# Identity multiplies on TensorE ahead of 22 waits in the first two sequences and the last one of a transformer block

## The reference, cut to what matters

```
x = x + attention0(layernorm(x))        # 16 heads of 8, full softmax, no output projection
x = x + ffn0(layernorm(x))              # 128 -> 512 relu -> 128
x = x + attention1(layernorm(x))        # 16 heads of 8, rotary, causal, output projection
x = x + local(layernorm(x))             # two layers; each: shift half of the features by a token,
                                        #   8 heads of 64 in a window of 64, then a gated gelu FFN
```

## Time and profile before

| what | us |
|---|---|
| median of 3 runs | 3026.3 |
| the profiled execution's own time | 3027.28 |
| its span, first to last instruction | 3025.5 |
| PE busy (share of the span) | 2775.7 (92%) |
| DVE busy | 2343.5 (77%) |
| ACT busy | 2138.3 (71%) |
| POOL busy | 1608.1 (53%) |
| mean granted clock of PE | 0.965 |

### The profile page before, as it was taken

The page is one execution under the profiler, slowest core; times in us unless marked ns, Lnnn a source line. Parts: engine busy times, 40 slices in busy tenths (PEclk is TensorE's granted clock), DMA queues, the critical chain, the costliest instruction groups (busy, mean ns, idle before and its releaser), DMA issues.

```text
span 3025.5 us, 66249 instructions
## 1 busy us (share of the span) xinstructions
PE 2775.7 (92%) x22656; PEld 1931.4 (64%) x22656; DVE 2343.5 (77%) x6016; ACT 2138.3 (71%) x5956; POOL 1608.1 (53%) x1747
## 2 busy tenths in 40 slices
PE   4688999999999999999999999999999999998875
PEld 2455666666676666666666666666666666666653
DVE  3467878888888888888888888887888888877753
ACT  2356777777777877777787777777777777776653
POOL 1045555566555556655555665555566555546642
PEclk7689999999999999999999999999999999999997
DMA  2000000000000000000000000000000000000000
GB/s 70 3 3 4 7 5 7 4 7 6 7 7 5 7 4 7 6 6 7 7 5 4 7 6 6 7 6 5 4 7 7 6 7 7 5 4 5 5 5 5
DMA packets 41976, 21.79 MB, mean 7 GB/s; under 512 B 21130, under 2 KB 41012, under 8 KB 41652
## 3 DMA queue, kind: packets, MB, share of 16 engines
q1 hardware_dynamic: 41652, 17.55, 2.1%
HBM read 9.17 MB, written 4.19 MB: 4 GB/s over the span
## 4 chain that ended last, share of the span: by engine, by line
PE 44%; ACT 23%; DVE 15%; POOL 7%; issue 3%; DMA 0%; DVEq 0%; POOLq 0%; SPq 0%; ACTq 0%
DVE negmax L864 7%; ACT P L756 6%; ACT rawP L756 6%; PE bank L1176 6%; PE bank L1192 5%; PE bank L1083 4%; PE bank L1184 4%; PE bank L1129 3%; PE bank L1118 3%; POOL rn L654 3%; PE bank L1163 3%; PE bank L1151 2%; ACT P L739 2%; PE bank L1063 2%; PE bank L1164 2%
## 5 line engine op out<-in xcount | busy, mean ns | idle before, releaser
L864 DVE TENSOR_REDUCE negmax<-bank 128x2 f32<-128x512 f32 (+1 forms) x896 | 559.9, 684 | 26.6 <-PE bank L1044 25.0
L723 ACT ACTIVATE probs<-bank 128x384 f32<-128x384 f32 (+1 forms) x1024 | 481.2, 581 | 110.3 <-PE bank L1063 109.1
L599 POOL TENSOR_TENSOR veps<-moments,eps_tile 128x2 f32<-128x2 f32 x192 | 38.4, 200 | 768.7 <-DVE moments L816 768.7
L1118 PE MATMUL bank<-wqkv_sb,hS 128*128 128x512 f32 x768 | 397.2, 625 | 27.0 <-DVE rawP L914 8.6
L621 POOL TENSOR_SCALAR_AFFINE_SELECT probs<-probs 128x256 f32<-128x256 f32 x512 | 245.9, 508 | 300.3 <-ACT probs L723 300.1
L654 POOL TENSOR_TENSOR rn<-ss_kept,minus_half 128x16 f32<-128x16 f32 x128 | 372.6, 2911 | 13.4 <-DVE ss_kept L921 12.8
L942 DVE TENSOR_REDUCE negmax<-bank 128x2 f32<-128x384 f32 (+1 forms) x384 | 212.9, 596 | 133.1 <-PE bank L1151 125.5
L1083 PE MATMUL bank<-probs,V 128*16 128x256 f32 (+1 forms) x4096 | 255.5, 369 | 24.8 <-ACT probs L723 22.8
L642 POOL TENSOR_TENSOR rawA<-rawA,rope_sb 128x512 f32<-128x512 f32 x128 | 164.6, 1286 | 168.4 <-ACT rawA L742 167.4
L1044 PE MATMUL bank<-kT,qT 32*128 32x256 f32 (+1 forms) x2048 | 213.4, 325 | 22.8 <-DVE negmax L864 17.2
L756 ACT ACTIVATE rawP<-bank,negmax 128x128 f32<-128x128 f32 x512 | 180.2, 378 | 66.8 <-DVE negmax L942 66.7
(11 more groups left out here) (139 smaller groups left out, 7283.4 us busy)
## 6 DMA issues: line engine op xcount, KB each, us to landing
xin<-x SPq DMA_DIRECT2D x32, 128.0 KB, 5.0
out<-xout SPq DMA_DIRECT2D x32, 128.0 KB, 1.8
V<-YB SPq DMA_DIRECT2D x64, 63.5 KB
wqkv_sb<-wqkv SPq DMA_DIRECT2D x1, 1536.0 KB
V<-YB SPq DMA_DIRECT2D x64, 0.2 KB
w_sb<-w SPq DMA_DIRECT2D x1, 682.0 KB
w_sb<-w SPq DMA_DIRECT2D x2, 256.0 KB, 3.0
wo_sb<-wo SPq DMA_DIRECT2D x2, 256.0 KB
```

The costliest lines, as they stand in the source:

```text
L723: nc.scalar.activation(dst, src, ACT.Exp, scale=SCALE0 if k == ATTN0 else SCALE1)\
L864: nc.vector.reduce_max(negmax[:, k, t, head:head + 4 * many - 3:4], tile(u, e)[:, :].rearrange("p (h k) -> p h k", h=many), AX.X, negate=T ...
L1118: mm(tile(u)[:], hS[:, l, t * P:(t + 1) * P], wqkv2_sb[:, l, m * INNER:(m + 1) * INNER], start=True, stop=True).then_inc(has_filled(u), 1)
```

## The change

A table gives a number of filler matmuls for 21 entries (sequence, stream, unit kind, part). Two entries match two units each (`turn_q` part 0, plain and with the maxima; `turn` of sequence 1, for the attention and for the FFN) and the very first `turn` of sequence 0 is left out. Ahead of such a unit PE waits until that unit's own bank is free, then multiplies the identity by four copies of itself (128x128 by 128x512, fp32r) into that bank as often as the table says, raising no semaphore. After that the unit waits for its inputs as before and overwrites the bank. There are 46 fillers in sequence 0, 48 in sequence 1, 22 in LOCAL0 and 70 in LOCAL1 of sequence 31, 186 in all.

```diff
+FILLERS = {
+    (0, ATTN0): {("turn_q", 0): 5, ("mix", 0): 7, ("mix", 1): 7, ("mix", 2): 7, ("mix", 3): 7, ("turn", 0): 8},
+    (1, ATTN0): {("turn_q", 0): 5, ("mix", 0): 7, ("mix", 1): 7, ("mix", 2): 7, ("mix", 3): 7, ("turn", 0): 5},
+    (31, LOCAL0): {("qkv2", 4): 6, ("scores2", 2): 6, ("turn_p", 0): 10},
+    (31, LOCAL1): {("qkv2", 2): 24, ("turn_q2", 0): 9, ("turn_p", 0): 9, ("turn", 0): 28},
+}
 NBANKS = 8
...
+                fillers = FILLERS.get((u.sequence, k), {}).get((u.kind, u.part), 0)
+                if fillers and (u.number > 2 or u.sequence > 0):
+                    for sem, count in newest(free(u)):
+                        pe.wait_ge(sem, count)
+                    for _ in range(fillers):
+                        mm(tile(u)[:].rearrange("p (a k) -> p a k", a=4), ident_r[:],
+                           ident_r[:].unsqueeze(1).broadcast_to([P, 4, P]), start=True, stop=True, skip_group_check=True)
+
                 if u.kind in ("turn", "shift"):
```

## The result

| kernel | median us | lowest and highest | runs | ratio to before, 95% interval |
|---|---|---|---|---|
| before, in these measurements | 3026.86 | 3024.83 to 3030.24 | 8 | |
| with the change | 3036.23 | 3028.83 to 3038.14 | 8 | 1.0027 [1.0016, 1.0038] |

What follows compares the result with a forecast made beforehand. PE bounds the whole span (92% busy), but where fillers lie no engine is full and a chain between engines counts. Sequences 0 and 1 about +1, the end +3.6: 3026.3 + 4.6 = 3030.9 us, range 3024 to 3038.

Steps and rivals of the forecast that it cites:

- The mechanism: In about half the places the bank holds the fillers back to the pause's end, so the pause stays.
- The price of a filler: On PE, each uncovered filler costs 0.427 us at half clock and 0.236 at full clock.
- Rival 2: Every filler shows its weight load, 0.315 or 0.575 us each: about +12 more, 3042 us; chance 0.15.
- Sequence 0, +5: Fillers of sequence 0 at the start cost about 5 us, passed on whole to sequence 1.
- sequence 1, -4.2: Most banks are free early in sequence 1; fillers cost little and full clock gives more back: sum -4.2 us.
- LOCAL0, +1.1: Sequence 31, LOCAL0: fillers of `qkv2` 4 +1.3, `scores2` 2 +1.42, `turn_p` 0 +0.1, return -1.7; net +1.1 us.
- what follows runs at full clock: -1.7: In LOCAL0, work behind the fillers of `turn_p` 0 was to run at full clock, returning 1.7 us.
- LOCAL1, +2.5: Sequence 31, LOCAL1: +1.9 up to the scores, `turn_p` 0 +2.5 less 1.4, `turn` -0.5; net +2.5 us.
- Rival 1: The clock stays up once the first fillers have run, in all four stretches: 3018.6 us; chance 0.15.
- Rival 3: The clock does not rise by fillers: sequence 0 +14, sequence 1 +5, the end +17, 3062 us; chance 0.05.
- Rival 4: Nothing shows: fillers lie under other work and the clock is unchanged, 3026 us; chance 0.1.
- Three signs named ahead: Sequence 1 later; 8.4 us pause ahead of the `qkv2` 2 fillers, `turn_q2` some 5 later; spacing 0.43 or 0.22 to 0.24.

Runs made afterwards that it cites:

- start alone: Changed kernel with only the fillers of sequences 0 and 1 kept, in their own banks: 3028.48 us against 3026.76 before, ratio 1.0002 [0.9992, 1.0012].
- the 24 in a free bank: Only the 24 fillers ahead of `qkv2` 2 of LOCAL1 kept, in the bank used longest ago: 3025.40 us against 3026.25 before, ratio 0.9996.

## Why the prediction was right in sign and short in size

**The mechanism: right.** The step was that a filler's own bank is freed by the releaser of the pause in about half the places. The rows after show it at each place named (17.97, 39.76, 2968.59), and the run with free banks changes nothing but the bank, and with it this wait, and moves the time from +0.3% to -0.4%. In LOCAL0 free banks take back only the cost of the six fillers of `qkv2` 4 (+0.2 for +1.3).

**The price of a filler: right.** Inside a chain of fillers the starts lie 0.427 us apart at half clock and 0.224 to 0.24 at full clock, which are the values taken. Only the first distance of a chain is longer, as a rule some 0.59 and 0.335. From the first of the 24 to the `qkv2` behind them are 7.56 us, with the clock rising during the tenth, and 6.96 in two other profiles, where it rises during the seventh. 7.4 was forecast with nine; that number had no row behind it, and it came out near. Rival 2, a load shown by every filler (0.575 and 0.315), falls: only the first distance of a chain is as long as that. The Trainium skill's figure of 131 ns for each pair of a sustained stream (same page, section Back-to-back issue gap) doesn't hold for these in fp32r: 0.224 is the smallest distance here.

**Sequence 0, +5, and sequence 1, -4.2: right as far as can be told.** Sequence 0 alone is +4.8 by its ratio, with 3 us on either side, and +1.6 to +5.6 in four profiles, of which up to 1.5 is the spread at that mark. Sequence 1 is -3.0 to -5.3 in the profiles. Their sum was forecast at +1; start alone is +0.6 by its ratio, with an interval of 3 us on either side.

**LOCAL0, +1.1: wrong, the step that failed.** It measured +5.6. Its parts:

| part | forecast | measured (three profiles) |
|---|---|---|
| six fillers of `qkv2` 4 | +1.3 | +1.2 to +1.4 |
| `scores2` 2 and `turn_p` 0, with what follows at full clock | -0.2 | +1.1 to +1.3 |
| one or both `up2` at half clock | 0 | +2.8 to +3.1 |

The fillers' own cost was about right again. What failed was the words "what follows runs at full clock: -1.7": in the second row 1.5 of cost stood against that return, and 1.1 to 1.3 is left; and in the third, what follows further on ran at half clock that had run at full clock before. The first is some 1.4 of the 4.5 us missed, the second some 3. The windows from mark to mark, LOCAL0 and then LOCAL1, in the profile of before:

```profile
2876.61:2957.70 81.09, 59.06 (x358) 40.36 (x356) 46.45 (x108) 42.34 (x124) 38.68 (x30) 0.92 0.02 5
2957.70:3021.92 64.22, 36.25 (x165) 23.87 (x164) 23.39 (x48) 22.43 (x62) 18.42 (x14) 0.71 0.01 4
```

and in the profile after:

```profile
2868.94:2955.62 86.68, 67.52 (x380) 46.58 (x378) 46.80 (x107) 42.09 (x124) 38.29 (x30) 0.90 0.02 5
2955.62:3023.56 67.94, 47.77 (x235) 34.32 (x234) 23.50 (x47) 21.76 (x62) 18.49 (x14) 0.85 0.01 4
```

In LOCAL0 the mean granted clock was 0.92 before, so there was little to win, and it is 0.90 after: the 22 fillers bought none, raising it in one place and losing it at `up2`. Free banks did not change that (0.92 and +5.1). In LOCAL1 it was 0.71 and is 0.85: there the 70 fillers bought clock, and lost more by standing behind their pauses; in free banks the same stretch has 0.91 and -5.1. I had read the pauses and not the mean clock of each stretch, which was there to be read before.

**LOCAL1, +2.5: short by 1.2 to 1.6.** 24 and 9 fillers up to the next scores measured +1.6 where +1.9 was forecast. `turn_p` 0 measured +1.3 to +1.8 for +1.1. The last `up2` measured +0.6 to +0.8 for -0.5: it takes 5.49 us behind 28 fillers, more than its 4.70 before. A row of the profile after shows it:

```profile
3015.11 5.49 PE L1206 MATMUL bank<-rawQ,w_sb 128*128 128x256 f32 x12 [0.66 <-ACT rawQ L689]
```

**The rivals.** Rival 1 needs the clock to stay up. It rose to 0.91 from 40 to 60 us and 0.86 from 100 to 120, and the kernel was still slower, so the clock did rise and its return was spent. With free banks the time goes beyond the rival's 3018.6, to 3012.8, though even there the clock doesn't stay up: it is 1.00 from 40 to 60 us and 0.66 from 80 to 100. Rival 3, no rise, falls by the same windows. Rival 4, nothing shows, falls by the end's +9.3.

Three signs named ahead came as forecast: sequence 1 began later in each profile with the fillers of sequence 0 in their own banks, 8.30 us of pause still stand ahead of the 24, and fillers lie 0.43 or 0.22 to 0.24 apart. `turn_q2` was to start some 5 us later behind its previous units; 2980.95 less 2968.59 is 12.4, against 7.6 before, so 4.7.

## What to carry to other kernels

Work that is put into a pause only to keep an engine's clock up must not wait for anything that ends the pause: look up who frees its buffer, and give it one that has been free for long. The buffer used longest ago is a good first choice, but not always free (3.21 us of waiting at one of 22 places here). That one choice was worth 0.7% here, made in two of the four stretches, and leaving out the part that loses another 0.1%. Before adding such work, read the mean granted clock of the stretch: near 1.00 there is little to win, and where the pause goes on after the last filler the clock can fall all the same.

## What the runs showed of the hardware that was not expected

- Stretches without any difference in their instructions differed by up to 9.3 us between profiles (201 to 2800 us), with the clock falling 13 times there in the profile of before, 9 in the one after, 14 in that of the same kernel again and 6 in that of the 24 in a free bank. A single profile of this kernel can't tell 0.2%.
- The clock fell in the 2.98 us behind a burst of 24 matmuls, at granted 1.00 just before, in two profiles. In the one of all fillers in free banks the same pause stands there, and the clock fell just behind it: the first two matmuls of `qkv2` 2 took 1.10 us and the next two 2.04. In both kernels with nine more fillers in the next pause it came back during these or right at their end (`turn_q2` takes 1.09 and 1.20 us).
- `up2` fell to half clock, in one unit or both and in part or whole, in six of six profiles with fillers in LOCAL0, 30 to 70 us ahead of it, in a stretch where before PE was busy 2.32 and 1.94 of 4.00 us and stayed at 1.00. More work ahead, and a lower clock behind: the cause stays open.
